# Values by seven block products over pairs of token tiles, and weight halves made on GpSimd

## The reference

```
xn = layernorm(x)
q, k, v = (einsum('bpd,hde->bphe', xn, W) + b for W, b in (Q, K, V))
scores = einsum('bqhe,bkhe->bhqk', q, k) / sqrt(128), causal
s = einsum('bqhe,hed->bqd', softmax(scores) @ v, W_O) + b_O
g = silu(((silu(xn @ gate_w.T * gate_s) * (xn @ up_w.T * up_s)) @ down_w.T) * down_s)
out = x + s * g
```

## Time and profile before

| | |
|---|---|
| three runs | 1110.94, 1112.88, 1117.75 us; median 1112.88 |
| profiled execution | 1109.62 us; span of its instructions 1107.7 us |
| granted TensorE clock | 0.999 of full speed |
| busy: PE, PEld | 1080.1 us (98%), 650.1 us (59%) |
| busy: DVE, ACT, POOL | 785.5 us (71%), 678.3 us (61%), 79.5 us (7%) |
| chain that ended last | PE 84%, DVE 5%, DMA 4%, ACT 3% |
| stretches | units begin at 275 us; FFN steps before |

### The profile page before, as it was taken

The page is one execution under the profiler, slowest core; times in us unless marked ns, Lnnn a source line. Parts: engine busy times, 40 slices in busy tenths (PEclk is TensorE's granted clock), DMA queues, the critical chain, the costliest instruction groups (busy, mean ns, idle before and its releaser), DMA issues.

```text
span 1107.7 us, 19624 instructions
## 1 busy us (share of the span) xinstructions
PE 1080.1 (98%) x6876; PEld 650.1 (59%) x6876; DVE 785.5 (71%) x1936; ACT 678.3 (61%) x1627; POOL 79.5 (7%) x108
## 2 busy tenths in 40 slices
PE   6999999999999999999999999999999999999998
PEld 3434444445656666666666666666666666666664
DVE  7766767665767777777777777777766666766676
ACT  6744454545667666766676666666666666556562
POOL 1000000001200000000000000000000000124433
PEclk9999999999999999999999999999999999999999
DMA  7435656577667767876886778668656667769875
GB/s 270 140 76 152 183 148 191 160 226 216 140 164 208 191 149 210 218 189 164 222 229 161 194 194 217 161 176 228 175 129 167 137 141 178 194 173 199 240 193 164
DMA packets 311291, 201.27 MB, mean 182 GB/s; under 512 B 251296, under 2 KB 279968, under 8 KB 310176
## 3 DMA queue, kind: packets, MB, share of 16 engines
q1 hardware_dynamic: 290272, 174.92, 62.0%
q10 hardware_dynamic: 17568, 14.16, 4.1%
q0 software_dynamic: 3360, 11.01, 3.1%
HBM read 106.73 MB, written 31.46 MB: 125 GB/s over the span
## 4 chain that ended last, share of the span: by engine, by line
PE 84%; DVE 5%; DMA 4%; ACT 3%; SPq 2%; issue 1%; POOL 0%; DVEq 0%; ACTq 0%
PE bank L625 76%; PE bank L786 9%; DMA arena<-arena 2%; DMA split_qk<-w_out 1%; ACT arena L1076 1%; DMA split_vo<-w_out 1%; SPq L415 1%; DMA b_o_rows<-b_o_dram 1%; DVE w_out L1162 1%; DVE arena L1269 1%; DVE arena L1264 1%; ACT arena L981 1%; DMA w_in<-attn_w_dram 1%; DVE arena L1148 0%; DVE arena L1207 0%
## 5 line engine op out<-in xcount | busy, mean ns | idle before, releaser
L625 PE MATMUL bank<-XT,arena 128*128 128x256 f16 (+2 forms) x1872 | 316.4, 314 | 2.7 <-issue 2.6
L625 PE MATMUL bank<-arena 128*128 128x512 f16 (+1 forms) x1124 | 276.4, 379 | 5.2 <-DVE arena L1269 4.9
L625 PEld LDWEIGHTS bank<-XT,arena 128*128 128x128 f16 (+1 forms) x1872 | 179.3, 98 | 112.2 <-issue 5.6
L1076 ACT ACTIVATE arena<-bank,neg_max 128x512 f32<-128x512 f32 (+3 forms) x256 | 132.7, 525 | 138.1 <-DVE neg_max L1397 138.0
L625 PE MATMUL bank<-ST,arena 128*128 128x256 f16 x1536 | 199.4, 273 | 1.4 <-DVE arena L1359 0.7
L625 PE MATMUL bank<-arena,XT 128*128 128x512 f16 x768 | 195.0, 379 | 0.7 <-issue 0.7
L625 PEld LDWEIGHTS bank<-arena 128*128 128x128 f16 x1124 | 107.4, 98 | 128.0 <-issue 13.9
L625 PEld LDWEIGHTS bank<-ST,arena 128*128 128x128 f16 x1536 | 147.9, 98 | 50.1 <-ACT arena L1051 4.0
L1397 DVE CUSTOM_DVE_ANT_0 bank<-bank,mask 128x512 f32<-128x512 f32 (+3 forms) x256 | 118.5, 517 | 39.1 <-PE bank L625 39.1
L1414 DVE SCALAR_TENSOR_TENSOR arena<-arena,inv_sum 128x512 f16<-128x512 f32 (+3 forms) x256 | 126.9, 557 | 3.6 <-ACT arena L1090 1.5
L1090 ACT ACTIVATE arena<-arena,inv_sum 128x512 f16<-128x512 f32 (+3 forms) x256 | 122.1, 551 | 0.0
(11 more groups left out here) (103 smaller groups left out, 1131.0 us busy)
## 6 DMA issues: line engine op xcount, KB each, us to landing
arena<-split_qk SPq DMA_DIRECT2D x64, 896.0 KB, 5.2
w_in<-attn_w_dram SPq DMA_DIRECT2D x64, 256.0 KB, 3.9
arena<-split_vo SPq DMA_DIRECT2D x8, 1024.0 KB, 6.8
split_qk<-w_out SPq DMA_DIRECT2D x30, 256.0 KB, 3.2
split_qk<-w_out ACTq DMA_DIRECT2D x26, 256.0 KB, 3.8
arena<-ffn_w_dram SPq DMA_DIRECT2D x8, 768.0 KB, 4.6
arena<-x_dram SPq DMA_DIRECT2D x20, 256.0 KB, 4.2
split_vo<-w_out SPq DMA_DIRECT2D x20, 256.0 KB, 4.1
```

The costliest lines, as they stand in the source:

```text
L625: mm = nc.tensor.matmul(out, stationary(a, k), moving(b, k), start=first and n == 0 and i == 0, stop=last and n == len(tiles) - 1 and i == ...
L1076: e = nc.scalar.activation(probs[:, at:at + width], SC[b_][:, col:col + width], ACT.Exp, bias=neg_max[:, i:i + 1], scale=-1.0, accum_out=r ...
```

## The change

- **V by block products.** V is computed for a pair of token tiles, p and p+2 of a batch, by the seven products over the same XT and ST rows, now as the stationary operand, with combinations of V's weights (256 columns) moving. 32 pairs take the place of 64 tiles. A pair spreads over two units: an odd u does products 1, 2 and 6 ("opening"), the next, even u 5, 7, 4 and 3 ("closing"). Pair p = (u+3)//2, so u = 60 has V too. Pair 0 and three products of pair 1 stand before unit 0.
- **Banks.** V's products use VB (as QB above) and the third score bank SC[2] (as KB). Each pair has three copies by ScalarE, three sums by VectorE, and three splits: first and second half of the first tile, and the whole second tile ("lower"). The first and the lower split read two SBUF tiles on VectorE, the second one a bank. `copies` is gone: sums are made in place, and its room holds V's sums.
- **Weights.** A group is now one run of 16 slots: seven combinations each for the two halves of query and key weights and for V's, and four rows of output weights, 25 splits for 22. ScalarE scales a loaded row in place first (`scale_weights`), and rounds without a scale. FFN steps keep 29 slots, with 44 splits for 38.
- **GpSimd.** In units 5 to 39 GpSimd makes the low halves and the sums, once the unit's last low key half is done (`keys_done`). In the FFN stretch VectorE does.
- **Buffers.** After the FFN stretch four buffers take split rows in turn; two of them lie in `down_rows` and `b_o_rows`.
- **SP.** A slot's stores and loads are issued one unit later, ahead of the transposes. V's weights load in three pieces, one or two units before use; two combinations lie in rows of XT that nobody reads any more.

```diff
-SLOTS = 8
+SLOTS = 16
+SLOT_SPLITS = [(0, (0,)), (0, (1,)), (0, (2, 3)), (0, (4,)), (0, (5, 6)),
+               (1, (0,)), (1, (1,)), (1, (2, 3)), (1, (4,)), (1, (5, 6)),
+               (2, (0,)), (2, (1, 2)), (2, (3, 4)), (2, (5, 6)),
+               (3, (0, 1)), (3, (2, 3))]
+SLOT_SUMS = {1: (0,), 2: (1,), 3: (2,), 4: (3,), 6: (0,), 7: (1,), 8: (2,), 9: (3,), 11: (0,), 12: (1, 2), 13: (3,)}
+SLOT_SCALES = {0: (0, 1), 1: (2, 3), 5: (0, 1), 6: (2, 3), 10: (0, 1), 11: (2, 3), 14: (0, 1), 15: (2, 3)}
+SLOT_LOADS = {3: (0, 1), 4: (3, 2), 8: (0, 1), 9: (3, 2), 12: (0, 1), 13: (3, 2), 14: (0, 1), 15: (2, 3)}
...
+OUT_OF = [n % 2 if n < FFN_SPLITS else (n - FFN_SPLITS) % 4 for n in range(len(SPLIT_ORDER))]
...
+        W_OUT = [w_out[:, 0:1024], w_out[:, 1024:2048], down_rows[:].bitcast(F16), b_o_rows[:].bitcast(F16)]
...  SP, loop over u
+                if LAG < u <= LAST_SLOT_UNIT + 1:
+                    weight_traffic(UNIT_SLOTS + u - 1)
                 transpose_probs(u)
...
-                slot = UNIT_SLOTS + u
-                if u >= LAG and slot < SLOTS * MACROS:
-                    weight_traffic(slot // SLOTS, slot % SLOTS)
...  GpSimd
+            def split_weights(slot):
+                g, i = divmod(slot, SLOTS)
+                j, splits = SLOT_SPLITS[i]
+                for e in splits:
+                    pool.wait_ge(w_hi, nth_split(g, j, e) + 1)
+                    nc.gpsimd.tensor_tensor(split_rows_out(g, j, e, 1), split_rows_in(j, e), split_rows_out(g, j, e, 0),
+                                            ALU.subtract).then_inc(w_lo, 1)
...
+            for u in range(LAG - 1, LAST_SLOT_UNIT + 1):
+                keys_done(u)
+                if u >= LAG:
+                    split_weights(UNIT_SLOTS + u)
+                if u < LAST_SLOT_UNIT:
+                    sum_weights(UNIT_SLOTS + u + 1)
...  TensorE
+            def v_product(p, name):
+                combo, rows, k0, half, to, first = PRODUCTS[name]
+                out = v_banks(p)[0 if to is QB else 1]
+                product(out[:, 0:HALF], lambda a, k: rows[a][:, (p // 2) % B, p % 2 + 2 * half, k0 + k, :],
+                        lambda b, k: WV[combo][:, k, b, :], range(2), first, True, partial=True).then_inc(vp_mm[name], 1)
...  unit, after P2
+                if v and opens:
+                    pe.wait_ge(wv_loaded[0], 16 * loads)
+                    pe.wait_ge(v_lo, 3 * p - 1)
+                    v_product(p, 1)
+                elif v:
+                    pe.wait_ge(wv_loaded[1], 48 * loads)
+                    pe.wait_ge(v_copied, 3 * p + 2)
+                    v_product(p, 5)
...  after P7
+                if v:
+                    pe.wait_ge(exp_ok, 2 * n)
+                    v_product(p, 2 if opens else 7)
...  after P5
+                if v and not opens:
+                    pe.wait_ge(wv_loaded[2], 48 * loads)
+                    pe.wait_ge(v_copied, 3 * p + 3)
+                    v_product(p, 4)
                 if v and out:
-                    project_v(u + 4, (3,))
                     project_out_tile(u - LAG, (0,))
...  after P3
+                if v and opens:
+                    pe.wait_ge(v_copied, 3 * p + 1)
+                    v_product(p, 6)
+                elif v:
+                    pe.wait_ge(v_sum, 3 * p + 2)
+                    v_product(p, 3)
...  before scores
+                if v:
+                    pe.wait_ge(v_sum, 3 * p + (1 if opens else 3))
...  ScalarE, unit
+                if v:
+                    copy_v(p, 0 if opens else 2)
+                if weights is not None:
+                    scale_weights(weights)
+                    split_weights(weights)
                 second_key_hi(n)
-                if v and u >= LAG:
-                    split_v(u + 4)
                 second_query_hi(n)
                 first_key_hi(n)
...
+                if v and opens:
+                    first_v_hi(p)
+                    copy_v(p, 1)
+                elif v:
+                    second_v_hi(p)
+                    lower_v_hi(p)
                 exps(n)
...  VectorE, unit
                 second_key_sum(n)
                 first_query_lo(n)
+                if v:
+                    sum_v(p, 0 if opens else 1)
                 second_key_lo(n)
                 second_query_sum(n)
                 second_query_lo(n)
                 first_key_lo(n)
+                if v and not opens:
+                    sum_v(p, 2)
                 if u > 0:
                     split_z(u - 1)
+                if v and opens:
+                    first_v_lo(p)
+                elif v:
+                    second_v_lo(p)
+                    lower_v_lo(p)
                 maxima(n)
```

More of the change, by code:

```diff
@@ L237, in out_bank, with v_banks @@
             return VB if t in (57, 59) else OB
-        def v_bank(t):
-            return SC[0] if isinstance(t, int) and t == 1 else VB
+        V_BANKS = {0: (SC[0], SC[1])}
+        def v_banks(p):
+            return V_BANKS.get(p, (VB, SC[2]))
         def xt_bank(k):
@@ L468, in _ @@
             turn_rows(0, XT, 1)
-            for j, b in ((0, 0), (1, 1), (2, 2), (3, 3)):
-                load_w(0, j, b)
+            for b in range(4):
+                load_w(0, b)
             for c in range(1, B):
@@ L482, in _ @@
                     if slot < FFN_SLOTS:
[L483 removed]
+                        weight_traffic(slot)
                     if m == 2:
@@ L996, in later_step, with weights @@
                 stores = m != 1 and 0 <= done < FFN_SLOTS
-                step(c, m, 2 if m == MT - 1 else m % 2, down_of=c - 1 if m == 0 else None,
-                     amid=(lambda: store_weights(done)) if stores else None)
                 slot = (MT - 1) * (c - 1) + m - 1
+                def weights():
+                    if stores:
+                        store_weights(done)
+                    if m > 0 and slot < FFN_SLOTS:
+                        scale_weights(slot)
+                step(c, m, 2 if m == MT - 1 else m % 2, down_of=c - 1 if m == 0 else None, amid=weights)
                 if m == 8 and c < B - 1:
@@ L1282, in later_step @@
                 if weighed:
-                    split_weights(*weights)
+                    split_weights(slot)
                 if m in (1, 2):
@@ L1429, in add_out, with unit @@
                                                op0=ALU.mult, op1=ALU.add).then_inc(out_added, 1)
-            def unit(u, v=True, out=True, weights=None):
-                n = u + 1
+            def unit(u):
+                n, p = u + 1, (u + 3) // 2
+                v, opens = p < V_PAIRS, u % 2 == 1
                 invert_sums(u, 1)
@@ L1471, in _ @@
             invert_sums(0, 0)
-            split_v(3)
             for u in range(NU - 1):
-                slot = UNIT_SLOTS + u
                 if u == LAG:
                     dve.wait_ge(acc_ready, T // P)
-                unit(u, v=u < 60, out=u >= LAG, weights=divmod(slot, SLOTS) if LAG <= u and slot < SLOTS * MACROS else None)
+                unit(u)
             invert_sums(NU - 1, 1)
```

475 lines of the change are left out of this document (287 added, 188 removed).

## The result

| | kernel before | kernel after |
|---|---|---|
| median of 12 runs | 1112.85 us (1109.79 to 1117.75) | 1119.30 us (1116.75 to 1122.18) |
| span of the profiled execution | 1107.7 us | 1117.3 us |
| mean granted clock | 0.999 | 0.992 |

The ratio is 1.0052, 95% interval 1.0036 to 1.0068. The forecast was 1104.5, its range 1094 to 1117.

The account below looks back on a forecast made before the run. Attention was taken as bound by TensorE's matmul columns, without gaps. Terms -16.4 (V products) + 9.0 (stalls) - 1.0 (FFN) = -8.4 us: profiled 1109.6 to 1101.2, stated as 1104.5 against the 1112.9 median; range 1094 to 1117.

Parts of the forecast that it names:

- Before unit 0 ... -1.2 with what follows: Prologue: ten V products (6.6 us) replace four tiles (10.4); scores start as now, P6 earlier, -1.2 us.
- Units 5 to 59: -16.7: Steady units before stalls: 28 opening at 12.40 and 27 closing at 13.05 us, against 55 at 13.02.
- stalls of +9.0: New waits in the attention units: 2.8 + 1.8 + 4.2 + 0.2 us, offsetting the saved columns.
- V4's wait: Closing units: product V4 waits for ScalarE's copy of V7 from the same bank, 0.10 x 28 = +2.8 us.
- The four ScalarE weight operations: Opening units 7, 19, 23, 35, 39: four weight operations ahead of the second key half delay scores 0.36, +1.8 us.
- The V split behind GpSimd: VectorE's V splits wait for GpSimd's operation on the shared port: +4.2 us via opening units, +0.2 in closing ones.
- GpSimd's operation: Weight split of GpSimd in units 5 to 39, taken as 1.26 us, with bounds 0.6 and 2.5.
- Rival 2: Under 1.21 us, GpSimd's second operation beats the lower V split: 0.65 x 18 closing units, +11.7, 1116 us; chance 0.16.
- DMA: nothing: Attention units: SP's earlier stores and loads, transposes landing in 4.3 us, and V's weights in three pieces cost nothing.
- Rival 3: Stores and loads hold up the transposes in 19 units with loads: +28 us, 1133; chance 0.07.
- FFN: -1: FFN stretch: more splits and scalings, but loads no longer behind the turning of rows; -1 us, bounds -2 and +3.
- Unit 60: +2.2: Unit 60 now closes the last V pair: 13.05 us against 10.88, +2.2.

Follow-up runs that it names:

- experiment 1: Kernel after without TensorE's second branch (whether FFN weights have low halves), always taking the two-pass arm: 1109.77 us, 0.9973 of the kernel before.
- experiment 2: Kernel before without TensorE's second branch, always taking the two-pass arm: 1111.46 us, 0.9989 of the kernel before.
- experiment 3: Kernel after, branch kept, with P4, P3 and V's product 2 of pairs 0 and 1 moved into both arms: 1116.2 us, 1.0033.
- experiment 13: Kernel before with its join moved ahead of the values of tiles 0 and 1, P4 and P3: 1116.62 us, 1.0026.
- experiment 10: Kernel after, branch kept, whole prologue and unit 0's first products in both arms, GpSimd's tail loads first, four FFN buffers: 1102.35 us, 0.9900.
- experiment 4: Kernel after with GpSimd's loads for units 56 and 57 issued ahead of its additions and products: 1114.97 us, 1.0012 of the kernel before.
- experiment 12: Kernel before without TensorE's second branch and with GpSimd's loads for units 56 and 57 first: 1108.44 us, 0.9968 of the kernel before.
- experiment 8: Kernel after without TensorE's second branch and with GpSimd's loads for units 56 and 57 first: 1103.85 us, 0.9916 of the kernel before.
- experiment 6: Kernel after with the second branch's two arms swapped and GpSimd's loads for units 56 and 57 first: 1109.05 us, 0.9972.
- experiment 7: Kernel before with GpSimd's loads for units 56 and 57 ahead of the finishing sums: 1109.03 us, 0.9972 of the kernel before.
- experiment 11: experiment 8 with VectorE instead of GpSimd making the weights' low halves and sums in units 5 to 39: 1106.13 us, 0.9934.
- experiment 14: experiment 10 with GpSimd instead of ScalarE scaling the arriving weight rows in the FFN stretch: 1108.61 us, 0.9957 of the kernel before.
- experiment 5: Kernel after with the second branch's arms in the other order, so the arm taken falls through to the join: 1113.9 us, 1.0008.

## Why the prediction was wrong, point by point

- **"Before unit 0 ... -1.2 with what follows" is the step that failed.** I walked the semaphore chain of the ten products and took it for the whole cost; the jump at the end of TensorE's arm I put at nothing, without a reason. It costs the kernel after 9.6 us (experiment 1) and cost the old one 0.9 (experiment 2). P4 and P3 moved from inside the arms to behind the join, and the last matmuls inside became short ones. The clue was in the timeline of before, a hole in the prologue that I passed over:

```profile
268.33 2.75 PE L625 MATMUL bank<-arena,XT 128*128 128x512 f16 x12 [0.69 <-issue]
```

  For each join, "cover" is the time from the start of the jump's record to the end of the last matmul that TensorE had queued ahead of it:

| kernel | jump's record | cover | hole | P1 to scores |
|---|---|---|---|---|
| before | 3.91 us | 3.4: P3 and 12 matmuls of 512 | 0.69 | 15.25 |
| experiment 3 | 4.29 | 2.1: P3 and 12 of 256 | 2.25 | 18.41 |
| after | 5.64 | 2.1: P5 and 12 of 256 | 3.59, then 3.43 | 24.46 |
| experiment 13 | 5.52 | 1.6: the last of the FFN and P5 | 3.98 | 19.87 |
| experiment 10 | 3.25 | 2.1: 18 of 256, and a wait that ends after 4.0 | none of its own | 14.83 |

  The hole is the record less its cover, to 0.2 us. The change cut the cover by 1.3 and lengthened the jump by 1.7; why a jump lasts 3.3 us in one place and 5.6 in another is open. The second hole, 3.43 here and 3.16 in experiment 4, has no branch record. A packet of instructions passes inside it, as inside the first, so I take both for instruction fetches that come too late. Behind the joins of the other kernels there is none; their blocks behind the join are longer (12 of 512, 18 of 256, against 6 of 256), but that this is the reason is not tested.

  The chain itself was wrong too, by less. With the branch out of both kernels (experiments 1 and 2), P1 of head 0 to the weighted values of unit 0 takes 29.59 us for 28.88, so +0.7 where I had -1.2. I had P6 of unit 0 come 0.8 earlier, because V no longer stands between ScalarE's exps and its copy of P1. It starts 5.68 after the first scores for 5.61: the exps begin 3.12 after them for 2.22. ScalarE's table load (1.28 us) now comes behind its wait for the first maximum, where it ran ahead of it in the old kernel. Timeline of ScalarE in experiment 1, then in experiment 2:

```profile
276.85 1.28 ACT L1221 ACT_TABLE_LOAD   x1 [1.56 <-DVE neg_max L1575]
...
272.06 1.28 ACT L1071 ACT_TABLE_LOAD   x1
```

- **"Units 5 to 59: -16.7" and stalls of +9.0**: together -7.7; the clean comparison (experiment 12 against 8) gives -9.4. Opening and closing units were right to 0.01 us, V4's wait included. The four ScalarE weight operations cost 0.70 in units 7, 23 and 39 and nothing visible in 19 and 35: 2.1 for 1.8. The V split behind GpSimd cost 1.5 us over all units, not 4.4.
- **GpSimd's operation.** Rival 2 hung on 1.21 us, and its condition came true: the weight split lasted 1.16, where my row of another shape had 1.26. The estimate of 1.12 worked out from the Trainium skill ("GPSIMD Engine Reference", performance versus the Vector engine) was nearer. The second weight split took the port 0.04 us ahead of the lower V split, which ended after 1.67 instead of 0.69:

```profile
547.48 1.17 POOL L622 TENSOR_TENSOR w_out<-w_in,w_out 128x512 f16<-128x512 f32 x1
...
547.52 1.67 DVE L1569 TENSOR_TENSOR V<-arena,V 128x512 f16<-128x512 f32 x1
```

  Its price was wrong, not its mechanism. Maxima do start late, but their delay mostly disappears in the next unit's slack. Thirteen of the 18 lower splits took 1.66 us or more, and the opening units behind them are 0.0 to 0.12 longer, not 0.65 (but for 7, 23 and 39 with their four weight operations, and 13, which has a collision of its own). Closing units behind an opening one whose first V split was late are 0.0 to 0.25 longer. That both operations exclude each other, as the Trainium skill ("SBUF — State Buffer", who interferes with whom) says of the shared port pair, agrees with these rows.
- **"DMA: nothing".** Nearly right in the units with weights: one unit (13) lost 0.91 there. Wrong in the tail: transposes and GpSimd's loads collided for +7.4 us over the two units, where the old kernel lost 2.0. Rival 3 had the mechanism and the wrong place. With the loads moved (experiments 4, 6, 8) units 57 and 58 are free of it, but some is left in all changed kernels: in unit 53, beside two loads of GpSimd that the old kernel has there too, the transposes take 5.3 to 8.4 us to issue (4.15 in the old kernel), and the unit 12.45 to 15.34 (13.29 in the profile after) for 12.40. Unit 13 takes 12.40 to 13.31. No run takes these apart.
- **"FFN: -1".** It is +1.7 in the profile after. P1 of head 0 starts at 255.2 to 256.9 in the five profiles with the old weight traffic (before, experiments 2, 7, 12, 13) and at 257.4 to 260.2 in the six with the new one and nothing else changed in the FFN (after, experiments 1, 3, 4, 8, 11): +2.8 on average. My bounds, -2 and +3, held it. Four buffers may give 0.7 of it back (1.4 of the median), within the noise, and ScalarE's scalings are cheaper where they are than on GpSimd (experiment 14). What the rest is, more splits or the later rows, stays open.
- **Unit 60: +2.2** was +2.3 with what follows it.

Against the forecast the spans miss by 18.0 (+9.6 for -8.4): 10.7 from P1 of head 0 to unit 4 (8.8 of it the jump, 1.9 the chain), 2.7 in the FFN, 4.5 in units 5 to 59 (the collision's 5.5 and unit 13's 0.9, less the 1.7 by which the units were better, and 0.2 of small differences), 0.1 behind them.

## What to carry to other kernels

Before moving work around a branch, look at what each engine has queued when it jumps, and for small holes marked "issue" behind the join: here 0.69 us was the visible end of a jump of 3.91. Ask the profile for the line of the branch and for the queue of instructions. In experiment 10 the join cost nothing, since it stood just ahead of a wait that was there anyway, with 2 us of matmuls queued before it. Compare a changed stretch with an old one that has been cleared of the same cost. And a forecast of the steady state, however exact, says nothing of the prologue and the tail: walk these two by resource too, not by semaphores alone.

## What the hardware showed that I had not expected

- A jump of TensorE over the other arm of a branch lasted 3.25 to 5.82 us in ten profiles, while the record of the same line that only enters the arm took 0.07. What was queued ahead of it went on meanwhile: with 3.4 us queued a hole of 0.69 was left, with 2.1 one of 3.59. Falling through from the last arm to the join cost nothing (experiment 5, the stretch 14.83 as without a branch), and so did a jump that ended 0.8 us before a wait did (experiment 10).
- A queue of its own brings TensorE's instructions in packets of 16 KB: three passed from 257 to 282 us in the kernel after, one from 260 to 285 in experiment 1. That this queue serves TensorE is my reading: its extra packets move with TensorE's jump (experiment 5).
- In a kernel whose granted clock is else 2.4 GHz, it fell to 1.2 within the first hole of the kernel after (0.50 from 266.7 to 277.0), with a single hole of 2.25 (experiment 3, 0.54 while the next 18 matmuls ran), and behind a wait of 5.20 (0.61 in the next 6 us). The matmuls there took up to twice as long, so a hole cost more than its length: 9.6 us for 7.0 of holes.
- GpSimd's subtraction with f16 operands takes 1.16 us against 1.26 with f32 ones; its multiplication by a constant takes 1.49 in the median of experiment 14 (1.59 on average), longer than the subtraction of two tiles.
- Two transposes took 9.26 us to issue beside four loads of 256 KB on GpSimd's queue, 4.6 to 4.8 without them (experiments 4, 6, 8).
